# Attention of a language-model tower: query and key projections as three float32r products, and a macro step in another order

## The chip, the core and the metric

The kernel runs on one NeuronCore of a Trainium2 chip. TensorE multiplies matrices, VectorE (DVE) and GpSimd (POOL) work elementwise, ScalarE (ACT) computes activations and copies, and SyncE (SP) issues the transfers here. All engines run at the same time and wait for each other by semaphores. The metric is the device time in microseconds (us); smaller is better.

## What is computed

Token rows are looked up in an embedding table and quantized (stage 1), go through causal attention with 12 heads of 64 columns (stage 2), and through a mixture of small experts (stage 3). There are 2 sequences of 2048 tokens with 192 columns. The change lies in stage 2:

```
q = jnp.einsum('bsd,hde->bshe', x, W_Q) + b_Q
k = jnp.einsum('bsd,hde->bshe', x, W_K) + b_K
v = jnp.einsum('bsd,hde->bshe', x, W_V) + b_V
scores = jnp.einsum('bqhe,bkhe->bhqk', q, k) / math.sqrt(D_HEAD)
scores = jnp.where(causal[None, None], scores, -jnp.inf)
pattern = jax.nn.softmax(scores, axis=-1)
z = jnp.einsum('bhqk,bkhe->bqhe', pattern, v)
attn_out = jnp.einsum('bqhe,hed->bqd', z, W_O) + b_O
```

## The kernel before

`stage_attention` goes through 12 **units**: 2 sequences by 6 pairs of heads. For a unit it needs queries, keys and values of both heads (projections, `project`), the largest score of every query row (`score_rows`, items called `s1`, whose results VectorE reduces in `take_maxima`, and `rows`, where they are transposed), and then the scores once more, transposed, with the maximum taken off (`score_columns`, items called `s2`). ScalarE takes their exponentials (`exponentials`), GpSimd adds these up (`acc`) for the denominators, and `weigh` multiplies them with the values. `add_up` (items `total`) sums the denominators over the partitions, VectorE inverts and multiplies (`invert`, `normalise`), and `output` (items `out`) applies W_O.

The scores of a unit are 40 **blocks** of 128 keys by up to 512 queries, two heads at a time. They are handled two by two in 20 **macro steps**. Beside unit n's blocks the projections and the first scores of unit n+1 are made: `PLAN[it][t]` lists the **items** of macro step t. Steps 1 and 2 hold a `q` and a `k` each, step 3 two `v`, steps 4 to 19 the 40 `s1` and 3 `rows`, and four `out` lie in steps 3, 5, 9 and 15. Unit 0's own projections and first scores run ahead of everything (`first_pass`).

The two results of a block, an item or a total go to a ring of three pairs of PSUM banks (`slot_free`, `order`, `place`): whatever is filled as number m waits until number m-3 has been taken by ScalarE or VectorE. The weighted values have two banks of their own.

Projections of queries and keys (L711, L714) are float32 matmuls. The 192 input columns are cut into 128 (`xt_hi`, `w_hi`) and 64 (`xt_lo`, `w_lo`). A float32 matmul stands in the profile as two MATMUL instructions. Scores are float32r: q and k are split into a high and a low part when they are evicted (`take_high` on ScalarE, `take_low` on VectorE), and three products are added (L727, L751), each one instruction for a head, after a product with a row of ones (L747).

The profile writes behind a matmul which part of the TensorE array it uses. Three **forms** matter: 128\*128, the whole array (first part of a projection, `out`, `rows`); 64\*128, half the rows, where the two heads run side by side (`s1`, `s2`, second part of a projection); and 128\*64, half the columns, again both heads side by side (`weigh` L767, `total` L781).

The order on TensorE in a macro step was:

```
score_columns(it, 2 * t)
score_columns(it, 2 * t + 1)
for item in PLAN[it][t]:
    side(item)
weigh(it, 2 * t - 2)
weigh(it, 2 * t - 1)
if behind(it, t, 1):
    add_up(*behind(it, t, 1))
```

## Time and profile before

| | |
|---|---|
| runs | 2645.27, 2647.95, 2650.46 us; median 2647.95 |
| profiled execution | 2648.46 us, of which the span from first to last instruction is 2646.7 |
| mean granted TensorE clock | 0.967 of full speed |
| attention's first matmul | 228.3 us after the start of the span |
| first pass of unit 0 | 67.1 us |
| unit 0 | 129.1 us |
| units 1 to 10 | 127.0 us each |
| unit 11 (no unit behind it) | 92.3 us |

A unit is counted here from its first `s2` matmul to that of the next unit. A row of the timeline gives a start, the time from it to the end of the group, engine, line, operation, output and inputs, the form and shape, how many instructions are merged, and in brackets the idle time before it. The ends of matmuls are modelled by the profiler, their starts are not: what TensorE spends is read from start to start (the **pitch**).

### The profile page before, as it was taken

What the parts mean: (1) busy time and instruction counts of PE and PEld (TensorE: products, weight loads), DVE (VectorE), ACT (ScalarE), POOL (GpSimd) and SP (SyncE); (2) the same over time, 40 slices, a digit from 0 to 9 for tenths busy, and PEclk for the clock granted to TensorE, in tenths of its full rate; (3) what the DMA queues carried; (4) which work ended last, traced back from release to release, by engine and by line L of the source; (5) the groups of instructions that cost most, each with busy time, mean ns of one, the idle gap of its engine ahead of it and who ended that gap; (6) DMA issues with size and microseconds to landing.
All of it is one profiled execution on the core that took longest, in us unless ns stands there. A gap on an engine that the chain in (4) does not pass through costs nothing. (4 is left out here: it accounts for less than half of the span.)

```text
span 2646.7 us, 42215 instructions
## 1 busy us (share of the span) xinstructions
PE 2390.5 (90%) x16000; PEld 1225.3 (46%) x16000; DVE 1859.5 (70%) x3771; ACT 1231.6 (47%) x1728; POOL 1242.6 (47%) x858
## 2 busy tenths in 40 slices
PE   3565899999999999999999999996999999999998
PEld 1233555555555555555555556543333333333332
DVE  7864565656565656566565656687988989888987
ACT  3422233333333333333333333354777777777776
POOL 5000265756575757575756666663413323324120
PEclk9787899999999999999999999996999999999999
DMA  1002000000001000000000001131011000000000
GB/s 50 12 23 61 1 8 8 3 9 1 10 1 33 1 10 1 10 1 10 1 9 1 3 1 20 19 53 55 9 19 21 15 19 21 15 19 9 19 7 7
DMA packets 42940, 39.33 MB, mean 15 GB/s; under 512 B 26865, under 2 KB 35186, under 8 KB 41842
## 3 DMA queue, kind: packets, MB, share of 16 engines
q1 hardware_dynamic: 40608, 31.18, 5.3%
q0 software_dynamic: 1536, 3.15, 0.4%
q8 instruction: 127, 2.08, 0.3%
q10 hardware_dynamic: 594, 2.31, 0.2%
q14 instruction: 75, 0.61, 0.1%
HBM read 26.13 MB, written 10.49 MB: 14 GB/s over the span
## 5 line engine op out<-in xcount | busy, mean ns | idle before, releaser
L678 POOL TENSOR_TENSOR acc<-acc,pT 128x1024 f32<-128x1024 f32 (+3 forms) x412 | 836.0, 2029 | 239.7 <-ACT pT L1077 202.9
L1077 ACT ACTIVATE pT<-banks 128x1024 f32<-128x1024 f32 x480 | 406.7, 896 | 812.9 <-PE banks L751 747.2
L1806 DVE TENSOR_TENSOR hw<-hid,banks 128x512 f32<-128x512 f32 x1024 | 662.8, 680 | 84.0 <-PE banks L1489 69.6
L896 DVE TENSOR_REDUCE part<-banks 128x2 f32<-128x1024 f32 (+3 forms) x432 | 438.0, 1044 | 313.0 <-PE banks L727 311.3
L1648 ACT ACTIVATE hid<-banks 128x1024 f32<-128x1024 f32 x512 | 496.7, 1022 | 183.8 <-PE banks L1479 167.4
L767 PE MATMUL banks<-pT,v 128*64 128x512 f32 (+3 forms) x1920 | 405.5, 543 | 1.1 <-POOL pT L662 1.1
L1489 PE MATMUL banks<-wT,select 64*128 64x512 f16 x1024 | 341.6, 392 | 42.1 <-DVE hw L1806 22.5
L1479 PE MATMUL banks<-zst,w1c 50*128 50x512 f32 x1024 | 306.5, 541 | 10.7 <-ACT hid L1648 10.7
L1497 PE MATMUL banks<-hw,w 128*32 128x512 f32 x2048 | 278.3, 616 | 0.8 <-DVE hw L1806 0.8
L1489 PEld LDWEIGHTS banks<-wT,select 64*128 64x128 f16 x1024 | 93.7, 94 | 399.1 <-DVE hw L1806 340.2
L767 PEld LDWEIGHTS banks<-pT,v 128*64 128x64 f32 x1920 | 116.7, 136 | 203.1 <-issue 181.1
L747 PE MATMUL banks<-zst,ones 64*128 64x512 f32 x960 | 199.9, 412 | 2.9 <-DVE h_all L954 2.7
L662 POOL TENSOR_SCALAR_AFFINE_SELECT pT<-pT 128x256 f32<-128x256 f32 x192 | 80.9, 421 | 246.1 <-ACT pT L1077 245.9
L727 PE MATMUL banks<-w1c 64*128 64x512 f32 (+3 forms) x1440 | 179.6, 380 | 9.2 <-DVE part L896 3.5
L751 PE MATMUL banks<-w1c 64*128 64x512 f32 (+3 forms) x1440 | 182.9, 362 | 0.0
L747 PEld LDWEIGHTS banks<-zst,ones 64*128 64x128 f32 x960 | 90.3, 184 | 197.9 <-issue 131.2
L939 DVE RECIPROCAL total<-total 128x256 f32<-128x256 f32 x96 | 167.5, 1745 | 3.1 <-ACT total L1085 2.7
L1389 POOL TENSOR_TENSOR o<-o,h_all 128x768 f32<-128x768 f32 x8 | 14.6, 1820 | 303.7 <-ACT o L1667 303.7
L727 PEld LDWEIGHTS banks<-w1c 64*128 64x128 f32 x1440 | 125.5, 190 | 49.0 <-ACT pT L1077 15.6
L1479 PEld LDWEIGHTS banks<-zst,w1c 50*128 50x128 f32 x1024 | 130.8, 192 | 17.5 <-ACT hid L1648 13.9
L751 PEld LDWEIGHTS banks<-w1c 64*128 64x128 f32 x1440 | 129.0, 186 | 17.9
L900 DVE CUSTOM_DVE_ANT_0 banks<-banks,mask 128x128 f32<-128x128 f32 x384 | 103.3, 311 | 29.5 <-PE banks L727 29.4
(228 smaller groups left out, 3161.4 us busy)
## 6 DMA issues: line engine op xcount, KB each, us to landing
zst<-z_scratch SPq DMA_DIRECT2D x48, 128.0 KB, 4.0
z_scratch<-zp SPq DMA_DIRECT2D x8, 512.0 KB, 2.8
out_h<-o SPq DMA_DIRECT2D x8, 384.0 KB, 2.6
xT_scratch<-xs_hi SPq DMA_DIRECT2D x4, 512.0 KB, 2.7
xt_hi<-xT_scratch SPq DMA_DIRECT2D x2, 1024.0 KB, 5.7
w<-in_L_ffn_W ACTq DMA_DIRECT2D x1, 2048.0 KB, 8.5
xt_hi<-in_L_ffn_W SPq DMA_DIRECT2D x12, 128.0 KB, 4.6
v<-in_L_ffn_W SPq DMA_DIRECT2D x12, 128.0 KB, 4.3
```

The source lines that it names most:

```text
L678: pool.tensor_tensor(acc[:, G % 2, :, off:CH], acc[:, G % 2, :, off:CH], pT[:, slot, :, 0:w], ALU.add).then_inc(summed, 1)
L727: last = pe.matmul(banks[h][:, 0:w], a[u][head(h), i * P:(i + 1) * P], b[u][head(h), c * CH:c * CH + w], start=(k == 0), stop=(k == 2))
L747: pe.matmul(banks[h][:, 0:w], ones[head(h), :], rows[head(h), u, Q, off:CH], start=True, stop=False)
L751: last = pe.matmul(banks[h][:, 0:w], a[u][head(h), kt * P:(kt + 1) * P], b[u][head(h), t0:t0 + w], start=False, stop=(k == 2))
L767: last = pe.matmul(psum[6 + G % 2][head(h), off:CH], v[:, u, kt, head(h)], pT[:, J % PSLOTS, h, 0:CH - off], start=(kt == 0), stop=(j == L ...
L896: last = dve.tensor_reduce(to[:, :, c:c + 1], both[:, :, 0:whole], AX.X, ALU.max)
L1077: act.activation(pT[:, J % PSLOTS, :, 0:CH - off], both[:, :, 0:CH - off], ACT.Exp, scale=E ** -0.5)\
L1479: last = pe.matmul(psum[i], w1[rows, s % NQ, j * P:(j + 1) * P], zst[rows, g % 2, s % NQ, :], start=True, stop=True)
L1489: pe.matmul(bank, select[rows, jr, :], wT[rows, g % 2, s, :], start=True, stop=True).then_inc(spread, 1)
L1497: last = pe.matmul(psum[Y][32 * i:32 * i + 32, :], w2[:, s, j, :], hw[:, n % 2, i, :], start=(n == 0), stop=(n == NSTEP - 1))
L1648: act.activation(hid[:, n % 2, 2 * pair:2 * pair + 2, :], banks[:, pair * 1024:(pair + 1) * 1024].rearrange("p (q n) -> p q n", n=GTOK), A ...
L1806: dve.tensor_tensor(hw[:, n % 2, q, :], hid[:, n % 2, q, :], ring_bank(("w", g, n, q)), ALU.mult).then_inc(mixed, 1)
```

## The change

1. **Projections of q and k** use float32r. ScalarE copies x and the weights of Q and K to a high part (`split_x_high`, `split_w_high`), VectorE subtracts that from the original (`split_x_low`, `split_w_low`), and TensorE adds three products for each of the two parts: high by high, low weights by high x, high weights by low x. The projection of values stays float32.
2. **Raw weights** have one buffer in place of two. Those of unit n+1 are fetched when unit n's projections have been taken, and are split in macro step 9 of unit n-1 (those of unit 1 after the first pass). The second x is split in steps 10 to 13 of unit 4.
3. **The macro step is woven**: block, first item, one weighting, block, second item, the other weighting, remaining items, total. ScalarE's order follows (exponential, first item, exponential, others).
4. Tiles: `oT` is gone (`normalise` writes in place into `total`, and `copy_total` now waits for the output product of two chunks before, not `normalise`), `ones_half` is a view of `ones`, the tiles of the last unit lie where the split x was, `idx` and `bo_bc` live in stage 1 only.

```diff
@@ sync: load_weights, and the loop over the units
-                    for dst, d0 in ((w_hi[:, u, k, :], 0), (w_lo[0:DLO, u, k, :], P), (w_lo[DLO:P, u, k, :], P)):
+                    for dst, d0 in ((w_hi[:, k, :], 0), (w_lo[0:DLO, k, :], P), (w_lo[DLO:P, k, :], P)):
...
             load_x(0)
+            load_weights(0)
             for n in range(2):
-                load_weights(n)
                 load_wo(n)
             for n in range(UNITS):
-                if n + 2 <= LAST:
+                if n + 1 <= LAST:
                     sp.wait_ge(low_taken, 4 * n + 4)
                     sp.wait_ge(v_taken, 2 * n + 2)
...
-                    load_weights(n + 2)
+                    load_weights(n + 1)
@@ tensor: project
                 if kind == "q" and c == 0:
+                    pe.wait_ge(w_low, 2 * n + 2)
+                if kind == "q":
+                    pe.wait_ge(x_low, (n // NP) * 4 + 2 * c + 2)
+                if kind == "v" and c == 0:
                     pe.wait_ge(x_in, (n // NP) * 48 + 48)
-                    pe.wait_ge(w_in[u], (n // 2 + 1) * 12 * 16)
+                    pe.wait_ge(w_in, (n + 1) * 12 * 16)
...
-                    for h in range(2):
-                        t = (2 * h + c) * CH
-                        pe.matmul(banks[h][:, :], w_hi[:, u, w, :], xt_hi[:, t:t + CH], start=True, stop=False)
-                    for h in range(2):
-                        part_rows = slice(h * DLO, (h + 1) * DLO)
-                        last = pe.matmul(banks[h][:, :], w_lo[part_rows, u, w, :], xt_lo[part_rows, c * CH:(c + 1) * CH],
-                                         start=False, stop=True)
+                    for k, (a, b) in enumerate(((wh_hi, xh_hi), (wl_hi, xh_hi), (wh_hi, xl_hi))):
+                        for h in range(2):
+                            t = (2 * h + c) * CH
+                            pe.matmul(banks[h][:, :], a[:, w, :], b[:, t:t + CH], start=(k == 0), stop=False)
+                    for k, (a, b) in enumerate(((wh_lo, xh_lo), (wl_lo, xh_lo), (wh_lo, xl_lo))):
+                        for h in range(2):
+                            part_rows = slice(h * DLO, (h + 1) * DLO)
+                            last = pe.matmul(banks[h][:, :], a[part_rows, w, :], b[part_rows, c * CH:(c + 1) * CH],
+                                             start=False, stop=(k == 2))
@@ tensor: the macro step
                     score_columns(it, 2 * t)
-                    score_columns(it, 2 * t + 1)
-                    for item in PLAN[it][t]:
+                    for item in PLAN[it][t][:1]:
                         side(item)
                     if t:
                         weigh(it, 2 * t - 2)
+                    elif it:
+                        weigh(it - 1, NK - 2)
+                    score_columns(it, 2 * t + 1)
+                    for item in PLAN[it][t][1:2]:
+                        side(item)
+                    if t:
                         weigh(it, 2 * t - 1)
                     elif it:
-                        weigh(it - 1, NK - 2)
                         weigh(it - 1, NK - 1)
+                    for item in PLAN[it][t][2:]:
+                        side(item)
@@ scalar and vector: the split
+            def split_x_high(b, k):
+                c, rest = divmod(k, 2)
+                act.wait_ge(x_in, 48 * b + 48)
+                if rest:
+                    cols = slice(c * CH, (c + 1) * CH)
+                    act.activation(xh_lo[:, cols], xt_lo[:, cols], ACT.Copy).then_inc(x_high, 1)
+                else:
+                    act.activation(half_view(xh_hi[:, :], c), half_view(xt_hi[:, :], c), ACT.Copy).then_inc(x_high, 1)
+
+            def split_w_high(n):
+                act.wait_ge(w_in, (n + 1) * 12 * 16)
+                for raw, high in ((w_hi, wh_hi), (w_lo, wh_lo)):
+                    act.activation(high[:, :, :], raw[:, 0:2, :], ACT.Copy).then_inc(w_high, 1)
...
+            def split_w_low(n):
+                dve.wait_ge(w_high, 2 * n + 2)
+                for raw, high, low in ((w_hi, wh_hi, wl_hi), (w_lo, wh_lo, wl_lo)):
+                    dve.tensor_tensor(low[:, :, :], raw[:, 0:2, :], high[:, :, :].bitcast(F32), ALU.subtract)\
+                       .then_inc(w_low, 1)
```

Where the order of instructions moves, two places show it. The first is TensorE in unit 5, macro step 13, a step with two `s1` items: L747 and L751 are a block (`s2`), L727 the items, L767 the weightings. In an order row the shape is the output's, and a float32 matmul is one instruction. Before:

```order
L747 MATMUL banks<-zst,ones 128x512 x2
L751 MATMUL banks<-qh,kh 128x512 x2
L751 MATMUL banks<-ql,kh 128x512 x2
L751 MATMUL banks<-qh,kl 128x512 x2
L747 MATMUL banks<-zst,ones 128x512 x2
L751 MATMUL banks<-qh,kh 128x512 x2
L751 MATMUL banks<-ql,kh 128x512 x2
L751 MATMUL banks<-qh,kl 128x512 x2
L727 MATMUL banks<-w1c 128x512 x12
L767 MATMUL banks<-pT,v 64x512 x4
```

And in the changed kernel, where L766 and L770 are a block, L746 an item and L786 a weighting:

```order
L766 MATMUL banks<-zst,ones 128x512 x2
L770 MATMUL banks<-qh,kh 128x512 x2
L770 MATMUL banks<-ql,kh 128x512 x2
L770 MATMUL banks<-qh,kl 128x512 x2
L746 MATMUL banks<-w1c 128x512 x6
L786 MATMUL banks<-pT,v 64x512 x2
L766 MATMUL banks<-zst,ones 128x512 x2
L770 MATMUL banks<-qh,kh 128x512 x2
L770 MATMUL banks<-ql,kh 128x512 x2
L770 MATMUL banks<-qh,kl 128x512 x2
L746 MATMUL banks<-w1c 128x512 x6
L786 MATMUL banks<-pT,v 64x512 x2
```

The four products of the two weightings stood together and now stand apart, each between products of the 64\*128 form.

The second place is TensorE in unit 5, macro step 1, around the query projection. Before (L751 ends block 3, L711 and L714 are `q` and then `k`, L767 the weightings):

```order
L751 MATMUL banks<-qh,kl 128x128 x2
L711 MATMUL banks<-xt_hi,w_hi 128x512 x2
L714 MATMUL banks<-xt_lo,w_lo 128x512 x2
L711 MATMUL banks<-xt_hi,w_hi 128x512 x2
L714 MATMUL banks<-xt_lo,w_lo 128x512 x2
L767 MATMUL banks<-pT,v 64x512 x2
L767 MATMUL banks<-pT,v 64x384 x2
```

Changed (L770 ends block 2, L729 and L733 are `q`, L786 is the weighting of block 0, L766 begins block 3):

```order
L770 MATMUL banks<-qh,kl 128x256 x2
L729 MATMUL banks<-xh_hi,wh_hi 128x512 x2
L729 MATMUL banks<-xh_hi,wl_hi 128x512 x2
L729 MATMUL banks<-xl_hi,wh_hi 128x512 x2
L733 MATMUL banks<-xh_lo,wh_lo 128x512 x2
L733 MATMUL banks<-xh_lo,wl_lo 128x512 x2
L733 MATMUL banks<-xl_lo,wh_lo 128x512 x2
L786 MATMUL banks<-pT,v 64x512 x2
L766 MATMUL banks<-zst,ones 128x128 x2
```

A projection of four float32 products has become one of twelve float32r products, and the key projection now comes after the next block.

## Rows read from the trace of the kernel before

**Rows 1.** Page, parts 1 and 2: engines over the whole span, and the granted clock.

```profile
PE 2390.5 (90%) x16000; PEld 1225.3 (46%) x16000; DVE 1859.5 (70%) x3771; ACT 1231.6 (47%) x1728; POOL 1242.6 (47%) x858
...
PEclk9787899999999999999999999996999999999999
```

**Rows 2.** Windows: length, then busy of PE, PEld, DVE, ACT, POOL; clock; first pass, units 0, 5, 11.

```profile
228.30:295.37 67.07, 57.39 (x348) 33.96 (x348) 49.75 (x114) 7.53 (x8) 0.00 (x0) 0.90 0.07 15
295.37:424.44 129.07, 124.80 (x862) 73.40 (x862) 72.96 (x136) 42.32 (x51) 82.35 (x56) 0.97 0.02 5
...
932.37:1059.36 126.99, 124.59 (x883) 73.98 (x882) 75.68 (x139) 42.66 (x52) 82.33 (x56) 1.00 0.03 5
...
1694.27:1786.60 92.33, 85.89 (x558) 45.27 (x558) 71.99 (x63) 46.30 (x54) 54.52 (x36) 0.99 0.30 51
```

**Rows 3.** Timeline, unit 4: TensorE pitches and both switches around a weighting.

```profile
913.58 0.40 PE L727 MATMUL banks<-kh,ql 64*128 64x512 f32 x2
...
913.91 1.94 PE L767 MATMUL banks<-pT,v 128*64 128x512 f32 x8
914.39 0.14 PEld L767 LDWEIGHTS banks<-pT,v 128*64 128x64 f32 x2 [0.28 <-issue]
914.82 0.14 PEld L767 LDWEIGHTS banks<-pT,v 128*64 128x64 f32 x2 [0.29 <-issue]
...
915.78 0.50 PE L747 MATMUL banks<-zst,ones 64*128 64x512 f32 x2
...
916.11 0.84 PE L751 MATMUL banks<-w1c 64*128 64x512 f32 x6
...
916.79 0.40 PE L747 MATMUL banks<-zst,ones 64*128 64x512 f32 x2
```

**Rows 4.** Timeline, TensorE, unit 6: one query item and the start of its key item.

```profile
1064.52 1.98 PE L711 MATMUL banks<-xt_hi,w_hi 128*128 128x512 f32 x4
1066.43 1.13 PE L714 MATMUL banks<-xt_lo,w_lo 64*128 64x512 f32 x4
1067.49 1.98 PE L711 MATMUL banks<-xt_hi,w_hi 128*128 128x512 f32 x4
```

**Rows 5.** Timeline, TensorE: full-height tiles, in the embedding and in an output item.

```profile
173.81 18.29 PE L378 MATMUL banks<-gates,steps_diag 128*128 128x512 f16 x84
...
999.42 1.57 PE L792 MATMUL banks<-wo,oT 128*128 128x192 f32 x8 [1.43 <-DVE part L896]
1000.92 1.94 PE L767 MATMUL banks<-pT,v 128*64 128x512 f32 x8
```

**Rows 6.** Waits of TensorE, units 1 to 10.

```profile
PE banks L792 <- DVE part L896: 14.4, 10, 1.5
PE banks L727 <- ACT pT L1077: 5.0, 20, 0.3
PE banks L792 <- DVE part L900: 3.0, 10, 0.3
```

**Rows 7.** Timeline, VectorE, unit 5, macro steps 8 and 9.

```profile
995.58 1.75 DVE L939 RECIPROCAL total<-total 128x256 f32<-128x256 f32 x1
...
998.14 2.36 DVE L896 TENSOR_REDUCE part<-banks 128x2 f32<-128x1024 f32 x2
```

**Rows 8.** Timeline, start of the attention: first transfer of weights, first matmul.

```profile
218.16 0.59 SPq L584 DMA_DIRECT2D w_hi<-in_L_attn_W_Q  x1
...
228.30 3.41 PE L711 MATMUL banks<-xt_hi,w_hi 128*128 128x512 f32 x4 [17.76 <-DMA bv_bc<-in_L_attn_b_V]
```

**Rows 9.** Groups by line and form: the nearest operations to the split.

```profile
L344 ACT ACTIVATE xs_hi<-banks 128x1024 f32<-128x1024 f32 x4 | 4.1, 1023 | 25.3 <-PE banks L390 25.3
L1101 ACT ACTIVATE w1c<-cpad 128x256 fp32r<-128x256 f32 x1 | 0.4, 410 | 0.0
...
L229 DVE TENSOR_TENSOR quant<-h_all,blk 128x1536 f32<-128x1536 f32 x4 | 7.0, 1758 | 0.1
L932 DVE TENSOR_TENSOR acc_odd<-acc_odd,pT 128x1024 f32<-128x1024 f32 x9 | 20.8, 2314 | 0.2
```

More of the change, by code:

```diff
@@ L780, in add_up @@
                     for h in range(2):
-                        last = pe.matmul(banks[0][head(h), :], ones_half[:, :], a[:, G % 2, h, :],
+                        last = pe.matmul(banks[0][head(h), :], ones_half, a[:, G % 2, h, :],
                                          start=(a is parts[0]), stop=(a is parts[-1]), skip_group_check=True)
@@ L791, in output @@
                 for t in range(TQ):
-                    last = pe.matmul(banks[t // 2][:, (t % 2) * D:(t % 2 + 1) * D], oT[:, G % 2, t * P:(t + 1) * P],
+                    last = pe.matmul(banks[t // 2][:, (t % 2) * D:(t % 2 + 1) * D], total[:, G % 2, t * P:(t + 1) * P],
                                      wo[:, u, :], start=True, stop=True, skip_group_check=True)
@@ L1026, in side @@
                     take_low(*item)
+            split_w_low(0)
+            for k in range(4):
+                split_x_low(0, k)
             rows_of_low()
@@ L1030, in _ @@
                 side(item)
+            split_w_low(1)
             for it in range(UNITS):
@@ L1034, in _ @@
                         side(item)
+                    if t == SPLIT_W_AT and it + 2 <= LAST:
+                        split_w_low(it + 2)
+                    if it == SPLIT_X_IN and t in SPLIT_X_AT:
+                        split_x_low(1, SPLIT_X_AT[t])
                     if it == LAST:
@@ L1083, in copy_total @@
                 if G >= 2:
-                    act.wait_ge(normalised, G - 1)
+                    act.wait_ge(filled, place[("out", (G - 2) // NQC, (G - 2) % NQC)] + 1)
                 act.activation(total[:, G % 2, :], both[:, 0, :], ACT.Copy).then_inc(total_copied, 1)
@@ L1114, in side @@
                     take_high(*item)
+            split_w_high(0)
+            for k in range(4):
+                split_x_high(0, k)
             for item in first_pass(0):
                 side(item)
+            split_w_high(1)
             for it in range(UNITS):
@@ L1120, in _ @@
                     exponentials(it, 2 * t)
+                    for item in PLAN[it][t][:1]:
+                        side(item)
                     exponentials(it, 2 * t + 1)
-                    for item in PLAN[it][t]:
+                    for item in PLAN[it][t][1:]:
                         side(item)
+                    if t == SPLIT_W_AT and it + 2 <= LAST:
+                        split_w_high(it + 2)
+                    if it == SPLIT_X_IN and t in SPLIT_X_AT:
+                        split_x_high(1, SPLIT_X_AT[t])
                     if behind(it, t, 1):
```

61 lines of the change are left out of this document (37 added, 24 removed).

## The prediction

> **What bounds the kernel now.** I read the parts of the profile in this order. First the engines over the whole span: TensorE is busy 90% of it, VectorE 70%, the others under half, and TensorE runs at its higher clock level, 2.4 GHz, in all but the first slices and one late one [rows 1]. Then the windows by unit: in unit 5 TensorE is busy 124.6 of 127.0 us, VectorE 75.7, ScalarE 42.7, GpSimd 82.3 [rows 2]. So units 1 to 10 are TensorE's, and the question is what it spends there. Unit 11 has 6.4 idle of 92.3 us. The first pass is different: TensorE idles 9.7 of 67.1 us behind VectorE's reductions, at a mean clock of 0.90.
>
> A busy share says little of matmuls that overlap, so I read starts. Two heads of a float32r product of 512 columns (64\*128 form) start 0.23 us after the two before them: three such pairs take 0.68 us, from 916.11 to 916.79 [rows 3]. A weighting is two float32 instructions per head, a pair every 0.43 us (914.39 to 914.82). But whenever the form of the tiles changes, both neighbours stretch. The last 64\*128 pair before a weighting takes 0.33 (913.58 to 913.91) in place of 0.23, the weighting's first pair 0.48 (913.91 to 914.39) in place of 0.43. The two pairs that follow 914.82 end at 915.78, in 0.96 in place of 0.86, and the first pair of the next block takes 0.33 (915.78 to 916.11). I call that a **switch**: into the 128\*64 form it costs 0.10 + 0.05 = 0.15 us, out of it 0.10 + 0.10 = 0.20 us. The projection shows the same between the other two forms: four instructions of 128\*128 last 1.91 us (1064.52 to 1066.43), 0.19 more than 4 x 0.43, and the 64\*128 pairs behind them 1.06 in place of 0.86 [rows 4]. The output item shows it too: eight 128\*128 instructions of 192 columns take 1.50 us before a weighting, 0.19 us each at most [rows 5].
>
> Semaphores don't explain it. Inside a projection no wait stands between the two parts, and still both sides stretch, while consecutive weightings wait for different exponentials and keep 0.43.
>
> **The weave.** It removes nothing from TensorE; it moves. In a macro step the two weightings stood together: one switch in, one out. Now each stands between products of another form. So every step has at least one more switch in and one more out, 0.35 us. I counted the changes of form in the whole order of both kernels. A unit from 1 to 10 has 63 before and 107 after; unit 0 has 60 and 103, unit 11 has 48 and 88. In all there are 523 more, 261 of them into the 128\*64 form and 262 into another. That is 261 x 0.15 + 262 x 0.20 = 39 + 52 = **+91.6 us**, or +7.7 us for a full unit. It lies wholly on the path, for TensorE is the engine that sets the unit's end.
>
> The Trainium skill has this rule: "Changing tiling mode (not just tile) drains the TensorE" (TensorEngine Tiling (Array Packing), Key Properties). It gives no price; the trace agrees, with 0.15 to 0.20 us a time [rows 3], and the rule speaks against this change.
>
> **The projections.** A q or k item lasts 2.97 us (1064.52 to 1067.49) [rows 4]: six float32 steps of 0.43, and 0.39 of switches. It becomes nine float32r steps, six of 128\*128 and three pairs of 64\*128, with the same switches. The trace of before has no float32r matmul of 128\*128. Its nearest rows: 64\*128 at 0.23 [rows 3]; 16-bit values in 128\*128 at no more than 0.218 (18.29 us for 84) [rows 5]; and as the upper end a first pair with its weights uncovered, 0.33 [rows 3]. I take 0.23, because float32 weights of full height are already hidden behind steps of 0.19 us [rows 5]. The item then costs 9 x 0.23 + 0.39 = 2.46 us, 0.51 less, and 48 items give **-24.5 us** (with 0.218 throughout -30, with 0.33 for the full-height ones +4).
>
> [...]
>
> **The waits.** The weave gives the ring more time, and some waits end. In ten units TensorE waits 14.4 us for VectorE before `out` in step 9, 5.0 us for exponentials and 3.0 us before the `out` of step 15 [rows 6]: 2.2 us a unit. That is a lower bound. With every pitch and switch of unit 5 added up at the prices above I get 122.7 us of 127.0 [rows 2], so 4.3 us are waits, the rest of them small ones inside `s1` items. The largest, 1.43 us in step 9, is VectorE's own queue: it inverts and normalises from 995.58, begins the step's first reduction only at 998.14 and ends it at 999.3 (half of 2.36), just before `out` starts at 999.42 [rows 5, 7]. From step 8's last `s1` to that point TensorE had 1.87 of weightings, 2.06 of blocks and 1.85 of `s1`, 5.8 us of work. In the new order it is no longer `out` but the third `s1` that needs the first one's bank pair, behind a block, `s1`, weighting, block, `s1`, weighting: 1.03 + 0.78 + 1.01 + 1.13 + 0.78 + 1.01 = 5.7 us of work. So that wait stays as it is, 1.4 us. Of the other 2.9 us I let nearly all go: **-2.7 us** a unit, -30 for 11 units, with 0.8 (only those that the view names, without step 9) and 4.3 as ends. In unit 11 a step has no `s1`; the weightings that move ahead cover waits for `normalise`. Of its 6.4 idle us I take **-5**.
>
> **The split.** In the steady units it is 2 copies of 256 columns on ScalarE (0.41 us each by L1101) and 2 subtractions on VectorE (0.39 us by L229 scaled to 256 columns and its fixed part, 0.6 by L932, which runs beside GpSimd) [rows 9]. They come behind step 9's items and are wanted in the next unit's step 1, over 60 us later; the 1.3 us of VectorE lie in a step where its next item is one reduction. Cost 0, at most 1 us for all units. The weights are fetched after step 3 and split in step 9, six steps or over 30 us later; from the first transfer's issue to the first use of a whole set it takes 10.1 us (218.16 to 228.30) [rows 8]. Nothing. At the start it is on the path. TensorE began at 228.30, when the last weight had landed [rows 8]. Now come two weight copies (0.8), a copy of 1024 columns of x (1.02 by L344), two subtractions of 0.39 beside it, and then those of x, 1.2 and 0.65 us (L229 scaled) [rows 9]. With ScalarE's first copy ended at 230.1, VectorE ends at 232.1: **+4 us** (2 to 6). TensorE's clock is at its low level when it begins, in either kernel, as the mean of 0.90 over the first pass says [rows 2].
>
> **Sum.** +91.6 - 24.5 - 30 - 5 + 4 = +36 us on the profiled execution's own 2648.5 us, which is 0.5 above the median of the runs: 2684. A full unit should go from 127.0 to 127.0 + 7.7 - 2.0 - 2.7 = 130.0 us.
>
> **Rivals.**
> (a) *The switches cost nothing when one weighting stands alone.* Then the weights of the next form would be loaded early, and only the gains are left: -24.5 - 30 - 5 + 4 = -56, 2593 us, faster. It decides at 0.17 x 523 against 56: if a switch costs under 0.11 us on average, the change gains. For it: nothing in the trace shows a single block between two `s2`. Against it: single `out` items and projections pay both sides [rows 4, 5]. The skill's sentence that the engine "pulls LDWEIGHTS ahead of in-flight MATMULs" (TensorE: Matmul & The Clock Gate, opening table) would give this result; the 0.33 us steps show that it does not hold across forms [rows 3].
> (b) *The waits stay.* VectorE's backlog behind each inversion (steps 1 to 4, 7, 8, 13, 14) meets a ring that now wants its `s1` results sooner after a block. Then -35 becomes 0 to -10 and the time is 2710 to 2720.
> (c) *Float32r of full height loads its weights uncovered*, 0.33 us: 0.10 x 6 x 48 = +29 on the sum, 2713.
> (d) *Every wait goes and the new products take 0.218*: +91.6 - 47 (11 x 4.3) - 6.4 - 30 + 2 = +10, 2658.
> (e) *The change doesn't do what it says*: single buffered weights arrive late for step 9 and ScalarE stands in front of the next exponential. A whole set took 10 us [rows 8]; 30 us are there. A stall would give 2700 or more.
>
> **Chances.** Forecast, 2665 to 2703: 0.60. (b) 0.12, (c) 0.07, (e) 0.02, all slower still. (d) or between it and the forecast 0.06, slower too. (a) or a part of it 0.13: 0.09 faster and 0.04 where half the price cancels the gains. Range 2658 to 2718, which leaves (a) and (e) out. A measurement of this kernel can tell 0.2% (5.3 us) from no change: slower 0.87, same 0.04, faster 0.09.
>
> **What would show it.** Units 1 to 10 last 130 us each, start to start, where they lasted 127.0, and unit 11 grows by about 2 us; the start of stage 3 is 36 us later and stage 3 is as long as before. A single weighting lasts 0.48 + 0.53 = 1.01 us, with 0.33 on both neighbours. A q item lasts 2.46 us. TensorE's 1.4 us wait in step 9 now stands before an `s1`. The first projection starts near 232 us. The forecast is wrong if a lone weighting lasts 0.86 with neighbours at 0.23, and wrong in size if a unit holds over 2 us of waits.

## The result, and the profile after

| | us, median of the runs | over the kernel before, with 95% interval |
| --- | --- | --- |
| before, beside the changed kernel | 2648.99 (2645.27 to 2650.46) | |
| changed | 2702.18 (2699.80 to 2703.74) | 1.0202 [1.0185, 1.0220] |

The change makes the kernel 53 us slower. The forecast was 2684 with a range of 2658 to 2718: the sign and the mechanism are right, the size is 18 us short. The profiled execution of the changed kernel has a span of 2699.9 us, 53.2 more than before.

The page of the changed kernel, parts 1 and 2: TensorE is busy 49.5 us longer, ScalarE 38 and VectorE 28, which have the split to do, and GpSimd 5 [rows 1]. The granted clock has the same digit in 39 of the 40 slices.

```profile
PE 2440.0 (90%) x16192; PEld 1228.5 (46%) x16192; DVE 1887.7 (70%) x3802; ACT 1269.7 (47%) x1760; POOL 1247.9 (46%) x858
...
PEclk9787999999999999999999999996999999999999
```

Windows of the changed kernel: the stretch and its length, then busy time of PE, PEld, DVE, ACT and POOL, the clock, and the DMA. They are the first pass, unit 0, unit 5 and unit 11, cut as in [rows 2], and last the whole of units 1 to 10.

```profile
232.22:298.28 66.06, 55.85 (x364) 37.25 (x364) 52.17 (x121) 8.16 (x11) 0.00 (x0) 0.88 0.04 8
298.28:428.97 130.69, 127.15 (x876) 73.78 (x878) 74.83 (x139) 44.81 (x53) 82.75 (x56) 0.99 0.02 4
...
953.54:1084.55 131.01, 128.93 (x898) 73.63 (x896) 77.46 (x140) 45.42 (x54) 82.72 (x56) 1.00 0.02 5
...
1740.12:1839.13 99.01, 92.94 (x558) 43.67 (x556) 72.46 (x63) 48.03 (x54) 53.85 (x36) 0.98 0.29 47
...
428.97:1740.12 1311.15, 1290.27 (x8962) 739.39 (x8960) 777.68 (x1402) 456.52 (x542) 828.66 (x560) 1.00 0.03 7
```

The same last window of the kernel before:

```profile
424.44:1694.27 1269.83, 1246.04 (x8804) 738.81 (x8802) 756.45 (x1381) 426.92 (x520) 823.53 (x560) 1.00 0.03 7
```

So the attention ends 52.5 us later, and this is where: it starts 3.9 later (232.22 for 228.30), the first pass takes 1.0 less, unit 0 takes 1.6 more, units 1 to 10 take 41.3 more (131.1 for 127.0 each), unit 11 takes 6.7 more. What follows is as long as before.

TensorE in the changed kernel, a single weighting between two `s1` items (start, length, operation, tiles, form):

```profile
940.22 0.43 PE L746 MATMUL banks<-kh,ql 64*128 64x512 f32 x2
940.58 1.08 PE L786 MATMUL banks<-pT,v 128*64 128x512 f32 x4
941.59 0.50 PE L746 MATMUL banks<-kh,qh 64*128 64x512 f32 x2
941.93 0.40 PE L746 MATMUL banks<-kl,qh 64*128 64x512 f32 x2
942.16 0.41 PE L746 MATMUL banks<-kh,ql 64*128 64x512 f32 x2
```

The weighting lasts from 940.58 to 941.59, 1.01 us for a pure 0.86, and its neighbours take 0.36 and 0.34 where a pair takes 0.23 (941.93 to 942.16). Both switches are paid again, as in [rows 3], with nothing hidden.

A query item of the changed kernel, and the weighting behind it:

```profile
959.97 0.72 PE L729 MATMUL banks<-xh_hi,wh_hi 128*128 128x512 f32 x2
960.53 0.62 PE L729 MATMUL banks<-xh_hi,wl_hi 128*128 128x512 f32 x2
960.99 0.63 PE L729 MATMUL banks<-xl_hi,wh_hi 128*128 128x512 f32 x2
...
962.45 1.08 PE L786 MATMUL banks<-pT,v 128*64 128x512 f32 x4
```

The item lasts 2.48 us (959.97 to 962.45), for 2.97 in [rows 4]. Two full-height products away from a switch take 0.46 (960.53 to 960.99), 0.23 each.

The two largest waits of TensorE in the changed kernel, units 1 to 10 (who waited, for whom, us in total, times, the longest):

```profile
PE banks L754 <- DVE cpad L956: 13.8, 10, 1.4
PE banks L746 <- DVE part L937: 4.6, 10, 0.5
```

Against [rows 6] the waits for exponentials are gone and the one in step 9 shrank from 1.4 to 0.5 us. But a new one stands at the top: 1.4 us in every unit before L754, which is `rows`, the first item of step 0. The names in the view are those of the last maxima. Here is that place in unit 5 of the changed kernel, and then the same place before (TensorE and VectorE, start and length, in brackets the idle time and what ended it):

```profile
953.34 0.39 PE L746 MATMUL banks<-kh,ql 64*128 64x512 f32 x2
...
953.77 0.96 DVE L937 TENSOR_REDUCE part<-banks 128x2 f32<-128x768 f32 x1 [0.46 <-PE banks L746]
...
954.25 0.40 PE L770 MATMUL banks<-qh,kl 64*128 64x512 f32 x2
...
955.71 0.17 DVE L956 TENSOR_TENSOR cpad<-negmax,cpad 128x8 fp32r<-128x8 f32 x1
...
956.03 0.63 PE L754 MATMUL banks<-ident,cpad 128*128 128x128 f32 x4 [1.38 <-DVE cpad L956]
```

```profile
930.40 0.39 PE L727 MATMUL banks<-kh,ql 64*128 64x512 f32 x2
930.72 1.73 PE L767 MATMUL banks<-pT,v 128*64 128x512 f32 x8
...
934.20 0.66 PE L735 MATMUL banks<-ident,cpad 128*128 128x128 f32 x4
```

From the last `s1` pair to `rows` VectorE needs 2.7 us (953.34 to 956.03) for its last reduction and the short chain behind it. Before, two weightings and two blocks lay in between, 3.8 us (930.40 to 934.20), and nothing waited. The weave moved the last `s1` behind the last weighting and `rows` ahead of the first, so only one block of 1.0 us is left as cover.

### The profile page after: what moved, and what is told of

It is laid out like the page before. It is cut to its first block and busy times, and to the rows that moved or that the text cites. A ratio compares the mean times of both kernels' runs of the same rounds, so it can differ in the third digit from the quotient of the medians.

```text
span 2699.9 us, 42687 instructions
## 1 busy us (share of the span) xinstructions
PE 2440.0 (90%) x16192; PEld 1228.5 (46%) x16192; DVE 1887.7 (70%) x3802; ACT 1269.7 (47%) x1760; POOL 1247.9 (46%) x858
## 5 line engine op out<-in xcount | busy, mean ns | idle before, releaser
L1138 ACT ACTIVATE pT<-banks 128x1024 f32<-128x1024 f32 x480 | 430.6, 897 | 867.1 <-PE banks L770 823.9
L937 DVE TENSOR_REDUCE part<-banks 128x2 f32<-128x1024 f32 (+3 forms) x432 | 448.2, 1047 | 337.9 <-PE banks L746 334.3
L786 PE MATMUL banks<-pT,v 128*64 128x512 f32 (+3 forms) x1920 | 456.2, 554 | 0.8 <-POOL pT L675 0.8
L766 PEld LDWEIGHTS banks<-zst,ones 64*128 64x128 f32 x960 | 89.9, 183 | 290.7 <-issue 259.1
L766 PE MATMUL banks<-zst,ones 64*128 64x512 f32 x960 | 216.7, 447 | 1.9 <-DVE h_all L993 1.7
L746 PE MATMUL banks<-w1c 64*128 64x512 f32 (+3 forms) x1440 | 195.2, 380 | 8.9 <-DVE part L937 6.4
L770 PE MATMUL banks<-w1c 64*128 64x512 f32 (+3 forms) x1440 | 186.4, 363 | 0.0
L746 PEld LDWEIGHTS banks<-w1c 64*128 64x128 f32 x1440 | 125.8, 189 | 71.5 <-issue 22.9
L786 PEld LDWEIGHTS banks<-pT,v 128*64 128x64 f32 x1920 | 95.1, 134 | 133.3 <-issue 109.3
L770 PEld LDWEIGHTS banks<-w1c 64*128 64x128 f32 x1440 | 129.8, 186 | 15.3
```

The costliest lines, as they stand in the source:

```text
L746: last = pe.matmul(banks[h][:, 0:w], a[u][head(h), i * P:(i + 1) * P], b[u][head(h), c * CH:c * CH + w], start=(k == 0), stop=(k == 2))
L766: pe.matmul(banks[h][:, 0:w], ones[head(h), :], rows[head(h), u, Q, off:CH], start=True, stop=False)
L770: last = pe.matmul(banks[h][:, 0:w], a[u][head(h), kt * P:(kt + 1) * P], b[u][head(h), t0:t0 + w], start=False, stop=(k == 2))
L786: last = pe.matmul(psum[6 + G % 2][head(h), off:CH], v[:, u, kt, head(h)], pT[:, J % PSLOTS, h, 0:CH - off], start=(kt == 0), stop=(j == L ...
L937: last = dve.tensor_reduce(to[:, :, c:c + 1], both[:, :, 0:whole], AX.X, ALU.max)
L1138: act.activation(pT[:, J % PSLOTS, :, 0:CH - off], both[:, :, 0:CH - off], ACT.Exp, scale=E ** -0.5)\
```

## The experiments

All kernels below were timed in rounds beside the kernel before. In all but the second the projections are the three-term ones of the changed kernel.

### One half at a time

The step order is undone and the projections kept. The function `parts` gives what goes between the blocks, behind the second block, behind the second weighting, and whether the weightings stand apart:

```diff
+        def parts(it, t):
+            return [], PLAN[it][t], [], False
...
-                order += [("s2", it, 2 * t)] + PLAN[it][t][:1] + [("s2", it, 2 * t + 1)] + PLAN[it][t][1:]
+                first, second, rest, split = parts(it, t)
+                order += [("s2", it, 2 * t)] + first + [("s2", it, 2 * t + 1)] + second + rest
...
+                    if not split:
+                        weigh_behind(it, t, 0)
+                        weigh_behind(it, t, 1)
```

> The changed kernel with the macro step of before (block, block, items, both weightings): projections, split and buffers changed, order not. Theory S (the loss is the 523 more changes of tile form, 0.15 to 0.20 us each, and the projections gain): a q or k item is 2.48 us in place of 2.97, 44 of them behind the first pass give -21, start and first pass +3 as in the changed kernel: about 2630 us, units of 125.1 us. Rival P (the float32r projections with their split are what costs, and the weave is neutral or gains): 2690 to 2710, units of 129 us or more. Rival M (half and half): about 2660.

Measured: 2629.96 us (2626.74 to 2631.96), ratio 0.9923 [0.9906, 0.9940].

The reverse, on the kernel before with its float32 projections:

```diff
+        def parts(it, t):
+            return PLAN[it][t][:1], PLAN[it][t][1:2], PLAN[it][t][2:], True
```

> The kernel before with the woven macro step and its order on ScalarE; projections stay float32. Theory S: changed kernel's 2702 plus what the projections give there, 21 - 3: about 2720 us, units of 133.0 us, a lone weighting 1.01 us. Rival P: at or under 2649.

Measured: 2719.00 us (2717.90 to 2719.97), ratio 1.0260 [1.0243, 1.0277].

So the projections give 19 us and the weave costs 70; together that is +51, and the changed kernel has +53. The two parts hardly touch each other. Units 1 to 10, projections alone and then weave alone:

```profile
421.29:1672.21 1250.92, 1226.82 (x8962) 762.47 (x8960) 767.48 (x1403) 435.55 (x542) 826.38 (x560) 1.00 0.03 7
```

```profile
427.90:1758.24 1330.34, 1309.48 (x8804) 716.92 (x8802) 766.68 (x1380) 447.96 (x520) 825.89 (x560) 1.00 0.03 7
```

A unit takes 125.1 and 133.0 us. Against 127.0 and 131.1 the weave costs 6.0 us in either arithmetic. Its 44 switches at the forecast's prices are 7.7, so the waits gave back 1.7 and not 2.7.

### The missed wait

In the changed kernel `rows` in step 0, and `out` in step 3 of unit 11, go behind the second block again, both weightings staying apart:

```diff
         def parts(it, t):
+            if t == 0 or (it == LAST and t == 3):
+                return [], PLAN[it][t], [], True
             return PLAN[it][t][:1], PLAN[it][t][1:2], PLAN[it][t][2:], True
```

> The changed kernel, but in step 0 the rows item, and in unit 11's step 3 the output item, are the second item, behind the second block, and no longer the first. Changes of form as in the changed kernel. The trace of the changed kernel shows TensorE waiting 1.4 us per unit at that rows item for VectorE's last maxima. Theory W (this is a wait of its own, made by moving the item forward): the 1.4 us go in 12 units and 1.7 in unit 11: 2702 - 18 = 2684 us. Rival: the wait only moves to the next block or weighting: 2698 to 2703.

Measured: 2682.52 us (2681.02 to 2683.60), ratio 1.0122 [1.0105, 1.0139], 19.7 us under the changed kernel, where 18 were expected. The largest wait of TensorE in its units 1 to 10:

```profile
PE banks L752 <- DVE part L949: 4.6, 10, 0.5
```

The 13.8 us are gone and nothing took their place: a unit lasts 129.7 us, 1.4 less, all of it in step 0. Unit 11 goes from 99.0 to 96.2: 1.4 in step 0 and 1.5 in step 3. The second is not the wait that I had expected to go. The weighting ahead of `out` now waits 2.3 us for the same normalisation that `out` had waited 2.4 for. In the changed kernel the clock stood at 1.2 GHz for 3.4 us from that place on (1757.0 to 1760.4), and here it doesn't fall. With this one item in its old place the kernel takes what the forecast had said of the changed one (2684), in part by luck: unit 11 is 2 us longer than forecast, and the first pass was 1.6 us shorter in this profile than in the changed kernel's, with the same instructions.

### Items between the blocks, weightings together

If the switches are the cost and the weave's distance is the gain, an item between the blocks with both weightings at the end should keep the gain at 774 switches (756 before):

```diff
         def parts(it, t):
+            return PLAN[it][t][:1], PLAN[it][t][1:], [], False
```

> The changed kernel, but both weightings stay together at the step's end: block, first item, block, other items, weighting, weighting. The ring of banks is filled in the order of the changed kernel, yet there are 774 changes of form, 18 more than before and 505 fewer than in the changed kernel. Theory S: the price of the forms goes, the gain of waits comes: -88 for the forms against the changed kernel, waits within 1 us per unit of the changed one: 2605 to 2620 us, units of 123 to 124. Rival O (what costs is the order of blocks and items in the ring, not the form): about 2700, as the changed kernel.

Measured: 2689.31 us (2687.24 to 2692.20), ratio 1.0152 [1.0135, 1.0169]. The theory of the switches alone fell here by 70 us: 59 us slower than the projections alone, with nearly the same switches. The largest wait of TensorE in units 1 to 10, and step 9 of unit 6:

```profile
PE banks L750 <- DVE part L947: 44.7, 40, 2.4
```

```profile
1137.68 1.75 DVE L990 RECIPROCAL total<-total 128x256 f32<-128x256 f32 x1
...
1139.22 0.40 PE L750 MATMUL banks<-kh,ql 64*128 64x512 f32 x2
1140.23 2.36 DVE L947 TENSOR_REDUCE part<-banks 128x2 f32<-128x1024 f32 x2
...
1141.51 0.33 PE L750 MATMUL banks<-kh,qh 64*128 64x128 f32 x2 [1.89 <-DVE part L947]
...
1141.99 2.58 PE L821 MATMUL banks<-wo,total 128*128 128x192 f32 x8
```

A window of the same kernel right behind it, columns as above:

```profile
1142.00:1144.40 2.40, 2.40 (x10) 2.07 (x8) 1.10 (x5) 0.00 (x0) 1.60 (x1) 0.58 0.00 0
```

The ring has three slots, so the third `s1` of a step takes the slot of the item three places ahead in the order. With the blocks side by side that is the second block, which ScalarE empties. With an item between them it is the step's first `s1`, which VectorE empties, and VectorE comes to it only after its reciprocal and the normalisation (1137.68 to 1140.15). TensorE stands from 1139.6 to 1141.5. The instructions that VectorE has ahead of that reciprocal were late too: a cast of 128 x 8 values lasts 1.06 us there, for 0.59 with the projections alone (more on it at the end). Then comes a second loss: the granted clock falls to 0.58 in the mean of the window above, which is 1.2 GHz for most of it, and `out` takes 2.58 us for 1.57 in [rows 5]. The trace has seven such short stretches in units 1 to 10, 24 us in all, each behind a wait of about 2 us; the kernel before, the changed kernel and the one with the projections alone have none there.

Against the projections alone units 1 to 10 lose 47 us: 25 are additional listed waits (47.5 for 22.7), 12 the clock (half of 24), 2 the switches, and 8 are not accounted for. Step by step the loss stands in the steps with three items, above all 14, 9, 11, 5 and 19. To test that it is VectorE's queue and not the distance alone, the same order with the reciprocals cut to 8 of 256 columns:

```diff
-                cols = slice(half * CH // 2, (half + 1) * CH // 2)
+                cols = slice(half * CH // 2, half * CH // 2 + 8)
```

> The run with items between the blocks (2689), but each of the 96 reciprocals inverts 8 columns in place of 256, so that VectorE's queue loses about 1.7 us in front of the reductions of steps 2, 3, 8, 9, 14 (most sums stay uninverted, so the attention's output is not normalised). Order, slots and switches stay. Theory V (the 5.2 us in a unit come from third items that wait for the slot of the first item, whose reduction stands behind VectorE's reciprocal and normalisation): most of the 5.2 goes in 11 units, and the 1.8 that `out` waits too: 2610 to 2630. Rival R (the short distance in the ring is enough by itself, one reduction being longer than the block and the item between): not under 2665.

Measured: 2631.53 us (2630.65 to 2632.15), ratio 0.9924 [0.9907, 0.9941]. The largest wait, units 1 to 10:

```profile
PE banks L750 <- DVE part L947: 13.8, 40, 0.9
```

58 us go with the reciprocals: 32 of listed waits (47.5 to 15.4), 12 of the clock (no stretch at 1.2 GHz is left in units 1 to 10), 4.5 in the tail, where the reciprocals are on the path themselves, and the rest in units 0 and 11. So with the reciprocals go about two thirds of what was waited and all of what the clock took; the time misses its range by 1.5 us. The rest of the waits is still VectorE's reductions, at the short distance. One control is missing. The order with the items together also waits for a reduction behind the same reciprocal (14.4 us at `out` in step 9), and it was not run with the short ones. So the runs show that most of this order's waits go with VectorE's reciprocals, and not how much of the 59 us between the two orders is theirs.

### The weightings elsewhere

Weightings apart, items together. The order of the ring is that of before, the switches are 1309:

```diff
+            return [blocks[0], sums[0], blocks[1], sums[1]] + items
```

> Three-term projections as in the changed kernel; a macro step is block, weighting, block, weighting, items. The items stay together and the order in which tiles take the PSUM ring is that of the kernel before, so only the number of form switches of TensorE changes against the kernel with the projections alone (2630): 1309 for 756, +553, of which 283 into the 128*64 form. Theory S (each switch costs 0.15 us into 128*64 and 0.20 into another form, wherever it stands): 283 x 0.15 + 270 x 0.20 = +96, so about 2726 (2715 to 2735). Rival O (the loss of the weave comes from the order in which the ring's slots come free, and switches are mostly hidden): 2630 to 2650.

Measured: 2812.18 us (2810.67 to 2814.21), ratio 1.0611 [1.0593, 1.0629], 86 us over the expectation. In the steps without a long wait (1, 2, 5 to 8, 13, 16, 18 and 19, mean of units 1 to 10) a pair of additional switches costs 0.26 to 0.51 us, 0.41 in the mean of the ten, where the prices say 0.35. The rest is again VectorE. Waits in units 1 to 10, and step 3 of unit 6:

```profile
PE banks L790 <- DVE total L986: 28.5, 10, 2.9
PE banks L821 <- DVE part L938: 25.0, 10, 2.5
PE banks L770 <- DVE part L938: 18.1, 20, 2.1
PE banks L758 <- DVE cpad L957: 9.7, 10, 1.0
```

```profile
1165.41 1.74 DVE L981 RECIPROCAL total<-total 128x256 f32<-128x256 f32 x1
1167.19 0.69 DVE L986 TENSOR_TENSOR total<-banks,total 128x512 f32<-128x512 f32 x1
...
1167.93 1.47 PE L790 MATMUL banks<-pT,v 128*64 128x512 f32 x4 [2.85 <-DVE total L986]
```

The first weighting of a query chunk goes to the bank of the chunk two before, and VectorE has yet to read and normalise what stands there. Behind the items it never waited; directly behind the first block it comes 2.85 us too early, in every unit. Units 1 to 10 take 166 us more than with the projections alone: 82 by the prices of 470 switches, 59 by listed waits (81.3 for 22.7), and 27 by the clock, which was low for 55 us in 15 stretches. That is 168, the whole. The 25.0 us before `out` in step 9 are not all order: the cast ahead of the reciprocal there lasts 2.09 us beside GpSimd's addition, for 0.60 with the projections alone.

Both weightings directly behind the second block, one item between the blocks, the rest at the end (827 switches):

```diff
+            return [blocks[0]] + items[:1] + [blocks[1]] + sums + items[1:]
```

> Three-term projections; a macro step is block, first item, block, both weightings, other items. Against the run with items between the blocks and the weightings last (2689), the third item of a step, which takes the slot of the first, has now two weightings more between itself and that first one. 827 switches, +71 against the order of before: +13. Theory R (the ring: the 2689 came from third items waiting for VectorE to reduce the first item of the same step, 5.2 us in a unit, at steps 5, 9, 11, 14 and 19): these waits are covered and the time is 2630 + 13, plus or minus 1 us in a unit of other waits: 2632 to 2655. Rival B (an item between two blocks costs by itself, by ScalarE's exponentials coming apart): as before, 2685 or more.

Measured: 2743.37 us (2741.94 to 2744.11), ratio 1.0351 [1.0334, 1.0369], about 100 over the expectation. My account of the ring was too simple: more distance between the first and the third `s1` of a step didn't help. Its largest waits in units 1 to 10:

```profile
PE banks L750 <- DVE part L938: 25.2, 11, 2.5
PE banks L758 <- DVE cpad L957: 19.3, 10, 1.9
```

The second is the `rows` wait again, now 1.9 us. The first is step 9 again. The weightings that were put between the first and the third `s1` were taken from between one step's last `s1` and the next step's, so VectorE gets its last reduction later. Work that is moved into one gap is taken out of another; what counts is where VectorE stands at that moment. But not all of it is distance: in step 9 of each of the eleven units with `s1` items the cast ahead of VectorE's reciprocal lasts 2.26 us, for 0.60 with the projections alone, and VectorE goes from it to the reduction that the third `s1` waits for without a pause. By that, 1.7 of the 2.5 us are this cast's (an estimate; the last section shows the cast). Units 1 to 10 lose 95 us to the projections alone: 41 by listed waits, 22 by the clock (13 stretches, 44 us), 11 by switches; 21 stay open.

Only the output item moved, behind the weightings, from the order of before:

```diff
+            if items[-1:] and items[-1][0] == "out":
+                return blocks + items[:-1] + sums + items[-1:]
+            return blocks + items + sums
```

> Step order of the kernel before with three-term projections (2630), but the output item of a step stands behind the weightings in place of ahead of them; the number of switches stays 756. At step 9 of each unit `out` waits 1.8 us for the slot of the first s1 item of its step; the two weightings (1.9 us) would now lie ahead of it. Theory R: the wait goes, -1.5 to -1.8 in 11 units: about 2612 (2608 to 2618). Rival: VectorE is the one in arrears, and the wait goes over to the next steps' items, which take the slots 2 us later: 2625 to 2635.

Measured: 2606.99 us (2604.76 to 2610.35), ratio 0.9843 [0.9826, 0.9859], 23 us under the projections alone for 18 expected, and 1 us under the stated range. The waits before `out` in step 9 (at most 1.5 us with the projections alone, not 1.8) and in step 15, which the expectation had left out, are gone and none came; by steps they give 1.5 and 0.4 us a unit. So units 1 to 10 take 123.2 us each, and this is all that TensorE still waits in them:

```profile
PE banks L752 <- ACT pT L1141: 4.8, 19, 0.3
```

### Fewer switches

The opposite of the weave, on that version: four weightings behind the items of every even step, none in odd ones, 565 switches:

```diff
+            sums = [] if t % 2 else [("sums", k) for k in (-2, -1, 0, 1)]
```

> The opposite of the weave, on the version with the output item last (2607): four weightings behind the items of every even step and none in odd steps. 565 switches for 756: 191 fewer, 119 of them into 128*64. Theory S: -119 x 0.15 - 72 x 0.20 = -32, about 2575 (2568 to 2585). Rival V (VectorE's queue): in odd steps only the next two blocks (2 us) lie between the last maxima of one step and the item that takes their slot, in place of 3.9 us, so 1 to 4 us of waits in a unit come: 2585 to 2620.

Measured: 2672.55 us (2671.26 to 2678.03), ratio 1.0083 [1.0066, 1.0101]: 66 us slower than with 191 switches more, and worse than either theory said. Its largest waits in units 1 to 10:

```profile
PE banks L763 <- DVE cpad L961: 19.2, 10, 1.9
PE banks L825 <- DVE part L942: 15.4, 10, 1.6
```

`rows` in step 0 has lost its cover of two weightings once more, and `out` in step 9 too. Listed waits are 58.6 us for 4.8, and the clock is low seven times again (12 us lost); with -28 for the switches that makes +38 of the +56 that units 1 to 10 show, and 18 stay open. Steps 3 and 4, 7 and 8, 17 and 18 lost nothing.

Projections in pairs (q with k of one chunk, both v), both full-height parts and then both half-height parts, 684 switches in the order of before:

```diff
+                        start_project(*item)
+                        start_project(*other)
+                        end_project(*item)
+                        end_project(*other)
```

> Step order of the kernel before with three-term projections (2630), and q and k of one chunk, and the two v items, done as one pair: both full-height parts, then both half-height parts. 72 switches of form fewer (684), all of the kinds that cost 0.20 us. Theory S: -72 x 0.20 = -14, about 2616 (2612 to 2622). Rival: the first of two is filled 1.2 us later and the second takes its slot 1.2 us earlier, so a wait for ScalarE's or VectorE's reading comes in two steps of each unit and eats 0.5 us or more of each: 2627 to 2640.

Measured: 2621.76 us (2619.82 to 2626.12), ratio 0.9899 [0.9881, 0.9917], 8 us of the 14. By steps, the first pair gives 0.38 us a unit, the v pair 0.21, the second pair 0.02.

With the output item last:

> Both edits together: projections in pairs (2622 alone) and the output item behind the weightings (2607 alone), against 2630 with neither. 684 switches. If they are independent: 2607 - 8 = 2599 (2595 to 2604). Rival: with the waits of step 9 gone TensorE comes earlier to the pairs and finds the slots taken, and the 8 us are lost: 2605 to 2610.

Measured: 2602.80 us (2599.67 to 2603.41), ratio 0.9812 [0.9796, 0.9828], 4 us for the pairs. The runs of one kernel differ by as much, so 4 and 8 us are not told apart; by steps the pairs give 0.38, 0.02 and 0.21 us a unit here as they did alone. What takes the gain of the second pair, in both kernels, is a new wait for the low parts of a query item, in five units under this name and in five under another (1.3 us):

```profile
PE banks L777 <- DVE ql L929: 1.7, 5, 0.6
```

On top of it four weightings at once, only in the three places that had borne it:

```diff
+            sums = [("sums", k) for k in (-2, -1, 0, 1)] if t in (4, 8, 18) else [] if t + 1 in (4, 8, 18) else sums
```

> On the version with pairs and output last (2603): the weightings of two steps stand together, four behind the items of the second, only in steps 3 and 4, 7 and 8, 17 and 18, where the run with four at once in all steps showed no wait, or one of at most 0.1 us, in the step that follows. 59 switches fewer (36 into 128*64): -36 x 0.15 - 23 x 0.20 = -10, about 2593 (2588 to 2597) by theory S with VectorE's queue out of the way. Rival V (any stretch without weightings brings VectorE's reductions into TensorE's way, in these steps too, or in step 9, where the reciprocal stands): 2600 to 2615.

Measured: 2593.31 us (2592.39 to 2596.93), ratio 0.9789 [0.9772, 0.9805]. It is the fastest of all, 56 us under the kernel before and 109 under the changed one. The three places give 0.15, 0.13 and 0.34 us a unit by the traces. What they don't give of 0.35 at steps 7 and 8 is a wait for ScalarE, here in unit 6 (the `s1` of step 7, the block of step 8):

```profile
1078.63 0.40 PE L758 MATMUL banks<-kh,ql 64*128 64x512 f32 x2
...
1078.99 0.19 PEld L778 LDWEIGHTS banks<-zst,ones 64*128 64x128 f32 x2 [0.40 <-ACT pT L1152]
1078.99 0.50 PE L778 MATMUL banks<-zst,ones 64*128 64x512 f32 x2
```

## Why the prediction was right, and what it missed

- **The price of a switch** held. A lone weighting lasts 1.01 us, as forecast, and the neighbours 0.33 to 0.36. +91.6 us was the right term. At each switch the load of the new form's weights starts with the new form's first matmul and not ahead of it (in [rows 3], 913.91 for both). The weave alone made the sum that the forecast has without the projections, +91.6 - 30 - 5 = +57, and measured +70; the 13 between them are waits. Rival (a), free switches, is dead: the trace shows every one of them paid.
- **The projections** held: an item fell by 0.49 us for 0.51. Alone they were to give -24.5 + 4 = -20.5 and gave -19. Rival (c), uncovered weights of full height, is dead (0.23 us, not 0.33), and so is (e): nothing waits for weights in step 9.
- **The start** held: first matmul at 232.22 for "near 232". (The terms written there, 230.1 + 1.2 + 0.65, add up to 232.0; the text has 232.1.)
- **The waits** are the step that failed, in three places. First, units 1 to 10 were to gain 2.7 us each and gained 1.7. The waits that I let go went, and more: the one in step 9, kept at 1.4, shrank to 0.5, because the step's items now lie apart and VectorE had caught up before them, and because the cast ahead of its reciprocal lasts 0.17 us for 0.60. Of what went, only a part is in the view: listed waits of units 1 to 10 are 22.4 us before and 20.8 after. Most of the other 1.5 us a unit were pairs inside `s1` items that lasted 0.05 to 0.12 us longer than 0.23 without a listed wait. Unit 5 has 14 of them before, 1.2 us in all, and 3 of 0.05 after. So the 4.3 us that the forecast had from its sum of pitches were there, for the most part. But I looked only for waits that the new order would take away and at the one I knew. `rows` became the first item behind the first block, while its input comes from the last item of the step ahead, which had moved behind the last weighting: 1.4 us, new, in every unit. The run with `rows` later showed it: 1.4 us in each of the 12 units, 16.8 of its 19.7.
- Second, **unit 11** was to grow by 2 us and grew by 6.7. Its 40 switches are +7.0, and the forecast's -5 for waits did not come. Its listed waits without the tail's are 6.8 us before and 6.8 after: small ones went, and `rows` came. Here are the three largest of unit 11 and the tail, and under them the wait for the normalisation before (the 5.1 us are the tail's in both):

```profile
PE banks L811 <- DVE total L985: 7.5, 2, 5.1
PE banks L766 <- DVE h_all L993: 1.7, 1, 1.7
PE banks L754 <- DVE cpad L956: 1.4, 1, 1.4
```

```profile
PE banks L792 <- DVE oT L946: 7.2, 2, 5.1
```

- The forecast's -5 rested on weightings that would cover waits for the normalisation. But in step 3 the rule that moved `rows` put `out` ahead of them, so it still waits for the normalisation, 2.4 us (7.5 - 5.1) for 2.1 before. In the run with `rows` later the first weighting stood ahead of `out` and covered nothing: it waited 2.3 us for the same event. Behind its wait of 2.4 us the changed kernel's clock fell for 3.4 us and took 1.5. The kernel before had one such stretch in this unit too, in step 19, and that one is gone.
- Third, the first pass gained 1.0 and not 2.0 us from its four items in this profile. That is mostly the clock. Nine kernels, the changed one among them, have the same first pass, instruction for instruction. It takes 65.9 to 66.1 us in the four profiles where TensorE was at 1.2 GHz for 16 us of it, the changed kernel's among them, and 64.4 to 64.8 us in the five where it was for 10 to 14 (67.1 before, with 13).
- **Sum by places**: 11 us short in units 1 to 10 (4.1 each for 3.0), 4.7 in unit 11, 1 in the first pass, 1.2 too much in unit 0; about 16 of the 17 us that the profiled executions show.
- Rival (b), waits that stay, had the right idea and the wrong place. It named VectorE's backlog behind the inversions; that decided three of the experiments, and not the changed kernel.

## What to carry to other kernels

When an order is changed by a rule for all steps (first item forward, last item back), list for every item what produces its input and what releases its buffer, and count the work that now lies between, above all at the seams where one step's last item feeds the next one's first. In this kernel TensorE is 98% busy in units 1 to 10, and yet two orders with nearly the same number of switches (756 and 774) differed by 59 us, with most of the difference in waits for one other engine's queue and in the clock behind them, and moving one kind of item behind the weightings gave 23. A wait of 2 us is dearer than it looks, since the clock may fall behind it. A switch of form costs 0.15 to 0.20 us here, and is worth removing only where the work that is moved for it was covering nothing.

## What the runs showed of the hardware

In none of the forecast's sums was there a term for the clock inside the units. It needs one when waits grow. Behind waits of at most 1.5 us (before, changed, projections alone) the granted clock of units 1 to 10 stayed at 1.00, 2.4 GHz. In four kernels waits grew to between 1.8 and 2.9 us, and behind some of these it fell to 1.2 GHz for a short stretch: 7 times in ten units with items between the blocks, 13 with both weightings behind the second block, 15 with the weightings apart and 7 with four weightings at once, for 12, 22, 27 and 12 us. The first of these has 20 such waits and only 7 stretches; which wait is followed by one, no run here shows.

A short VectorE instruction can last thirteen times its usual time. In the run with both weightings behind the second block, the cast of 128 x 8 values takes 0.18 us in the median of 48 and 2.27 at most, and the long one is this (VectorE and GpSimd, unit 6):

```profile
1170.18 2.38 POOL L695 TENSOR_TENSOR acc<-acc,pT 128x1024 f32<-128x1024 f32 x1 [1.01 <-ACT pT L1139]
1170.32 2.27 DVE L956 CAST cpad<-negmax 128x8 fp32r<-128x8 f32 x1
```

It starts 0.14 us behind GpSimd's addition and ends with it, at 1172.6 (1170.32 + 2.27, and 1170.18 + 2.38). It is no accident of one place. In the traces of all fourteen kernels 319 of these casts start inside a GpSimd TENSOR_TENSOR, and every one of them ends 0.03 or 0.04 us behind it, after 0.26 to 2.29 us by how far the addition had come; the 251 that overlap no GpSimd instruction at their start take 0.17 or 0.18 us. Before the change the cast of step 14 starts 0.86 us into an addition and lasts 1.57 us, in the changed kernel 1.32 into it and 1.10. So a small shift of GpSimd's work changes how long VectorE takes, and in some orders TensorE's waits with it, as in step 9 of this run. The orders shifted the two engines against each other and the duration followed each time; no run took GpSimd's addition away. The Trainium skill says that VectorE, in some of its modes, and GpSimd take one pair of SBUF ports as "an exclusive lock, not a bandwidth split" for a whole instruction (SBUF — State Buffer, SBUF: two separate sides); this trace agrees, with 2.27 us beside 0.18.

The third thing is that even a very short wait has a cost, listed or not. In the last profile above the `s1` pair ahead of the waiting block takes 0.36 us and the block's first pair 0.34 by the pitches of its step, as around a switch, though both have the same form. The weights of the block could not be fetched while it waited. So a wait too short to be listed still costs 0.1 us, and that is why removing a switch that covered such a wait gave 0.13 us and not 0.35.
